# Edge scatter of a four-layer graph network: places settled and handed over two chunks at a time instead of four

## The reference, cut to what matters

```python
bias = jnp.full((n, n), NEG, dtype=x.dtype)
bias = bias.at[diag, diag].set(0.0)
bias = bias.at[dst, src].set(edge_weight.astype(x.dtype))
...
scores = jnp.einsum('hnd,hmd->hnm', q, k) / np.sqrt(HEAD_DIM)
scores = scores + bias[None, :, :]
attn = jax.nn.softmax(scores, axis=-1)
```

## Time and profile before

| what | value |
|---|---|
| median of 3 runs | 583.27 us (582.19 to 585.47) |
| the profiled execution | 581.37 us, of which span 579.6 us |
| busy: PE, DVE, ACT, POOL | 530.0, 396.6, 225.9, 282.2 us |
| mean granted clock of TensorE | 0.973 |
| scatters (L387, POOL) | x68, 75.1 us busy, mean 1105 ns, idle before them 40.4 us |
| one-hot builds (L1131, L1132, DVE) | x68 each, 407 and 609 ns |
| marks (L1114, DVE) | x68, 609 ns |
| one-hot matmuls (L521, PE) | x544, 119.5 us |

### The profile page before, as it was taken

The page is one execution under the profiler, slowest core; times in us unless marked ns, Lnnn a source line. Parts: engine busy times, 40 slices in busy tenths (PEclk is TensorE's granted clock), DMA queues, the critical chain, the costliest instruction groups (busy, mean ns, idle before and its releaser), DMA issues.

```text
span 579.6 us, 7779 instructions
## 1 busy us (share of the span) xinstructions
PE 530.0 (91%) x2524; PEld 351.7 (61%) x2524; DVE 396.6 (68%) x939; ACT 225.9 (39%) x473; POOL 282.2 (49%) x271
## 2 busy tenths in 40 slices
PE   6999999999969999898899999997998997999880
PEld 2444444448845545666677888877876785555750
DVE  6996979999947769974676744464427626774846
ACT  2120530017227662574441233143534226765443
POOL 6557556668457777404342600066653654766000
PEclk8999999999989999998999999998999999999996
DMA  7940000000665210226632500028652852100001
GB/s 239 400 151 1 1 1 0 0 0 2 198 199 166 55 37 1 73 60 157 213 115 82 178 31 1 0 81 248 182 182 73 259 171 69 47 2 1 0 0 73
DMA packets 29913, 54.37 MB, mean 94 GB/s; under 512 B 4962, under 2 KB 6446, under 8 KB 29368
## 3 DMA queue, kind: packets, MB, share of 16 engines
q1 hardware_dynamic: 15964, 27.14, 15.0%
q0 software_dynamic: 11968, 19.96, 11.5%
q10 hardware_dynamic: 1948, 6.86, 3.5%
HBM read 51.78 MB, written 2.17 MB: 93 GB/s over the span
## 4 chain that ended last, share of the span: by engine, by line
PE 47%; DVE 10%; ACT 5%; POOL 5%; DMA 4%; issue 3%; ACTq 0%; DVEq 0%; POOLq 0%
PE bank L498 9%; PE bank L499 8%; PE bank L500 8%; PE bank L616 4%; PE bank L600 4%; PE bank L591 3%; POOL wl L346 3%; DMA wh<-w_o 2%; PE bank L693 2%; PE bank L691 2%; PE bank L692 2%; DVE h L1084 2%; DVE h L1083 1%; PE bank L568 1%; PE bank L484 1%
## 5 line engine op out<-in xcount | busy, mean ns | idle before, releaser
L346 POOL TENSOR_TENSOR wl<-wraw,wh 128x512 fp32r<-128x512 f32 (+1 forms) x78 | 105.4, 1372 | 81.1 <-ACT x L811 14.9
L521 PE MATMUL bank<-hot 128*128 128x512 bf16 x544 | 119.5, 383 | 2.5 <-DVE hot L1132 2.5
L521 PEld LDWEIGHTS bank<-hot 128*128 128x128 bf16 x544 | 53.5, 99 | 68.7 <-DVE hot L1132 4.1
L387 POOL DMA_INDIRECT edge_bias<-ewn,cell_at x68 | 75.1, 1105 | 40.4 <-issue 20.2
L498 PE MATMUL bank<-wh,tl 128*128 128x512 f32 x176 | 71.3, 405 | 0.6 <-DVE tl L1043 0.5
L499 PE MATMUL bank<-wl,th 128*128 128x512 f32 x176 | 69.4, 395 | 0.0
L500 PE MATMUL bank<-wh,th 128*128 128x512 f32 x176 | 69.4, 394 | 0.0
L819 ACT ACTIVATE sp<-sp,peak 128x512 f32<-128x512 f32 x44 | 31.8, 722 | 26.4 <-DVE peak L1255 26.1
L1132 DVE TENSOR_SCALAR hot<-iota,pair_dst,digit 128x1024 bf16<-128x1024 f16 x68 | 41.4, 609 | 0.0
L498 PEld LDWEIGHTS bank<-wh,tl 128*128 128x128 f32 x176 | 33.5, 190 | 11.8 <-issue 4.2
L1114 DVE SCALAR_TENSOR_TENSOR eq<-keyb,key,later 128x384 f16<-128x384 f16 (+1 forms) x68 | 39.8, 609 | 0.0
(11 more groups left out here) (194 smaller groups left out, 1072.2 us busy)
## 6 DMA issues: line engine op xcount, KB each, us to landing
wraw<-w SPq DMA_DIRECT2D x26, 256.0 KB
wh<-w POOLq DMA_DIRECT2D x6, 1024.0 KB, 6.1
keyb<-edge_keys ACTq DMA_DIRECT2D x4, 1088.0 KB, 11.4
wh<-w_rel POOLq DMA_DIRECT2D x4, 1024.0 KB, 5.8
wraw<-w_rel SPq DMA_DIRECT2D x16, 256.0 KB
wraw<-w_qkv SPq DMA_DIRECT2D x8, 256.0 KB
wraw<-w_o SPq DMA_DIRECT2D x8, 256.0 KB
wh<-w_o POOLq DMA_DIRECT2D x2, 1024.0 KB, 8.0
```

The lines of the kernel that those rows point to most:

```text
L346: pool.tensor_tensor(wl[n % WSLOTS][:, k, 0:width], wraw[:, q % 3, 0:width], wh[n % WSLOTS][:, k, 0:width], ALU.subtract).then_inc(s["w_lo ...
L387: pool.indirect_dma_start(out=bias_dram, out_offset=bass.IndirectOffsetOnAxis(ap=cell_at[:, c:c + 1], axis=0), in_=ewn[:, c:c + 1], in_off ...
L521: mm = pe.matmul(ps(name)[:], hot[:, slot, 0, i * P:(i + 1) * P], hot[:, slot, 1 + kind, :], start=False, stop=last, skip_group_check=True)
```

## The change

Places are settled for two chunks at a time. In `build_and_place` the first two chunks of a group are settled behind the build of slot 2, the other two where all four were settled before. In the code between and behind the loops a settle stands behind each second mark. `dups` is raised at each second mark, and GpSimd waits for `placed` ahead of each second scatter. So 34 settles of two columns stand in place of 17 of four.

```diff
@@ GpSimd
             for c in range(CHUNKS):
-                if c % GROUP == 0:
-                    pool.wait_ge(s["placed"], c // GROUP + 1)
+                if c % 2 == 0:
+                    pool.wait_ge(s["placed"], c // 2 + 1)
                 if c >= WINDOW:
                     pool.wait_ge(scattered[c % WINDOW], 16 * (c // WINDOW))
@@ VectorE
             def mark(c, k):
 
                 ins = later_same(c + k, k)
-                if k == GROUP - 1:
+                if k % 2 == 1:
                     ins.then_inc(s["dups"], 1)
 
-            def settle(c, group):
-
-                dve.wait_ge(s["dups"], group + 1)
-                dve.scalar_tensor_tensor(out=cell_at[:, bass.ds(c, GROUP)], in0=dup[:, bass.ds(c, GROUP)], scalar=OUT_OF_RANGE,
-                                         in1=key[:, bass.ds(c, GROUP)], op0=ALU.mult, op1=ALU.add).then_inc(s["placed"], 1)
+            def settle(c, group, half):
+
+                dve.wait_ge(s["dups"], group * 2 + (half + 1))
+                at = c + 2 * half
+                dve.scalar_tensor_tensor(out=cell_at[:, bass.ds(at, 2)], in0=dup[:, bass.ds(at, 2)], scalar=OUT_OF_RANGE,
+                                         in1=key[:, bass.ds(at, 2)], op0=ALU.mult, op1=ALU.add).then_inc(s["placed"], 1)
@@ build_and_place
                     build_chunk(at + (first + slot), slot)
+                    if slot == 2:
+                        settle(c, group, 0)
                     mark(c, slot)
                 mark(c, RING - 1)
                 dve.wait_ge(s[f"hot_used{sweep}"], at)
                 build_chunk(at + (first + RING - 1), RING - 1)
-                settle(c, group)
+                settle(c, group, 1)
@@ between the loops
             for k in range(GROUP):
                 mark(behind, k)
-            settle(behind, behind // GROUP)
+                if k % 2:
+                    settle(behind, behind // GROUP, k // 2)
@@ behind the second loop
             for c in range(behind + CBLOCKS[1] * RING, CHUNKS, GROUP):
                 for k in range(GROUP):
                     mark(c, k)
-                settle(c, c // GROUP)
+                    if k % 2:
+                        settle(c, c // GROUP, k // 2)
```

## The result

The changed kernel took 579.92 us (median of 20 runs, 575.76 to 584.59 but for one run of 676.88 us), the kernel before, on the same chip, 583.28 us (20 runs). The ratio is 0.9931 with a 95% interval of 0.9908 to 0.9955, which is 4.0 us less (the medians differ by 3.4 us). The profiled execution took 581.01 us, of which 579.3 us are span.

A forecast was written before the change was run, and what follows sets the result against it. The end of GpSimd's scatters was taken to set the attention's start. 2.1 us from the scatters plus 0.5 us from TensorE's clock made 2.6 us off 583.27 us: 580.7 us, range 578.4 to 582.9 us.

The forecast's parts named there:

- rival A: The forecast itself: 1.5 to 3.5 us gained, 579.8 to 581.8 us; chance 0.50.
- rival B: Last scatters fall out of step with VectorE's counts, or the low clock goes wholly: likelier 3.5 to 5.5 us; chance 0.20.
- The 4.26 us: GpSimd's "issue" wait ahead of the load of `w_o`: taken to hang on the bias's landing and move along.
- Rival D: The 4.26 us wait ends at a fixed place and takes up the gain: 0 to 0.5 us, about 583.2 us; chance 0.12.
- The scatters: GpSimd's last scatters, freed by an earlier settle, end 2.1 us earlier; bounds 1.3 and 4.7 us.
- A gain of 2.1 us passes whole: From the scatters' end to the attention's first `scale_rows`: the whole 2.1 us arrives, being under the 4.7 us limit.
- 4.7 us of room: Before the attention: `scale_rows` could start 4.7 us earlier before TensorE's last product of v and first inverse limit it.
- The clock: TensorE's low clock at the attention's start: less work at half pace, 0.5 us gained; bounds 0 and 1.9 us.
- VectorE's settles: 17 more settles on VectorE: hidden in the loops' waits; counts and q start 0.1 to 0.2 us later.
- My sign for a higher price: One-hot matmuls ending more than 0.5 us later than about 129.8 us would show VectorE pays more than said.
- Rival C: Scatters among VectorE's builds: the two moved and the next two pay 0.5 us each, about 582.5 us; chance 0.14.
- Rival E: The settle in the loop body holds VectorE up, 1.2 us a round: slower, 586.7 us; chance 0.04.

The follow-up runs named there:

- padded change: The changed kernel with 112 more GpSimd semaphore increments that nobody waits for, making its program 128 instructions longer than the kernel before: ratio 0.9948.
- pads in both directions: Unread GpSimd increments added: 112 to the changed kernel (wait back, ratio 0.9948), 16 to the kernel before (wait gone, 0.9929).
- kernel with settles and waits: The changed kernel's two-chunk settles and 16 added GpSimd waits, but waiting for the same counts as before, so no scatter freed earlier: ratio 1.0023.
- kernel with more settles and no earlier scatters: The changed kernel's two-chunk settles with no scatter freed earlier: ratios 1.0061 and 1.0013 with GpSimd's old waits, 1.0023 with 16 more waits.
- waits alone: The kernel before with GpSimd waiting for `placed` ahead of each second scatter, for counts already there, and no added settles: ratios 0.9911 and 0.9953.
- moving the banks: VectorE reads count banks 4 to 7 before unpacking them: in the changed kernel 0.9943; in the kernel before with the 16 waits 0.9897 (577.92 us).
- before plus 16: The kernel before with 16 GpSimd semaphore increments that nobody waits for, between two pieces of its first `low`: ratio 0.9929.
- kernel with the first loop as before: The changed kernel with the first loop settled four chunks at a time as before, and as many GpSimd waits as the change: ratio 0.9938.

## Why the prediction was right, and where not

The forecast was 580.7 us, 0.45% less; measured were 0.69% less, inside the range of 578.4 to 582.9 us. The forecast of the median was 0.8 us off (579.92 us measured), but the size came out near by other steps, so its closeness is in part luck. The median lies at the lower edge of rival A, the 4.0 us of the ratio in the likelier part of rival B (3.5 to 5.5 us), and both things that B named happened: scatters got faster, and the low clock went wholly.

| scatters / GpSimd's fetch | behind the bias's load | moved out of its way |
|---|---|---|
| as before | 1 | 0.9929; 0.9911, 0.9953 |
| as before, with the added settles | 1.0061, 1.0013 | 1.0023 |
| freed earlier, with the added settles | 0.9948 | 0.9931, 0.9933 |

Against the kernel before, each of the two alone gives 0.5 to 0.9%, and both together no more. The padded change is the kernel that the forecast described: earlier scatters, and the wait still there. It gave 0.5% (0.1 to 0.9), where 0.45% was forecast.

- **The 4.26 us: wrong, and the main miss.** The step was "so I take the wait to hang on that landing, and to move along". It went with GpSimd's own instruction fetch, and the change moved the place of that fetch in the program by 16 instructions. I wrote that each second scatter's wait costs "nothing"; as waits that is so, but as instructions they took 4.3 us out. Rival D (a fixed place) had the same flaw: both moved or held the wait, neither removed it. That GpSimd's program length decides is shown, by the pads in both directions. That the packet is what GpSimd waits for is inferred, from its place in each case and from the 1.50 us that always lie between its end and the next instruction: no record links the two. That it takes long because of the bias's load is argued only: no run changed that load.
- **The scatters: right in mechanism, too small.** The first half was settled 1.87 us ahead of the second (1.94 said). But the last 12 also ran faster, 17.5 us in place of 19.0: four of 1.50 us in a row, and only 0.97 to 1.14 us in the eight others. Measured against the one-hot matmuls the end came 3.5 us earlier, not 2.1. In the span's own time it was 1.8 us, only because the sweeps were 1.7 us late in that execution.
- **"A gain of 2.1 us passes whole", "4.7 us of room": wrong.** The room was not fixed. The earlier `low` pieces fell on a count of VectorE that stands ahead of a bank read that k needs, and v came 1.8 us later. Of the 7.9 us at `w_o` 3.0 us passed. What I had named as the limit above ("TensorE's last product of v") was the bound.
- **The clock:** I took 0.5 us, with 1.9 us as the bound if no work runs low. TensorE's idle time shrank to 0.51 us and the clock did not fall there, so this came out at its bound, in both profiles. The reading behind the 0.5 us was sound: in the kernel with settles and waits the idle time was 3.32 us and one low stretch of 3.4 us followed (180.2 to 183.6 us), as expected for 3.3 us. What failed is the idle time that it was given.
- **VectorE's settles:** 0.1 to 0.2 us were said. The second sweep lasts as long as before (62.0 us from first to last weight load in both), and the first is within what it varies by. My sign for a higher price, one-hot matmuls more than 0.5 us later, did appear (1.7 us), but the second profile of the kernel before has them 3.3 us later than its first: the sign could not tell. What I had not costed is their shift against the scatters: it shows only where no scatter is freed earlier, as one scatter of 3.9 us.
- **Rival C:** the moved scatters took 1.14 and 1.10 us, not 0.5 us each more. Rival E: no held-up loop; the kernel with more settles and no earlier scatters is slower by 0.1 to 0.6%, of which only the 0.6 is clear of its interval, and what its profiles show of it is in the tail. For the count of 4.76 us beside three `low` pieces the Trainium skill ("SBUF — State Buffer", "Who interferes with whom") has a rule that fits: a VectorE instruction with two SBUF inputs contends with a GpSimd instruction that reads SBUF. For the 3.9 us scatter it does not settle the matter: the same section tells of a probe in which `tensor_tensor` did not stall a DMA, while here a scatter took 3.90 and 3.91 us beside four of them, in all three profiles with settles and no earlier scatter.
- Of my tests, "`w_o` near 152.4 us" and "TensorE's idle time is near 3.2 us" failed, on the good side: 148.30 and 0.51 us. "Last scatter ends at 141.5 to 142.4" held (142.27), but only since the later sweeps and the faster scatters cancelled.

What stays open: why VectorE stalls for 1 to 8 us between 46 and 61 us in all these kernels, and the end of the sweeps moves by up to 5.4 us between two executions of one program (135.5 and 130.1 us with the waits alone); why the vanished wait gives no time where the settles stand and no scatter is earlier; and whether moving the banks gains, which needs finer timing than 0.4%.

## What to carry to other kernels

A gap labelled "issue" in front of an instruction that waits for nothing may be the engine's own program arriving: look in the DMA rows for an instruction packet just ahead of its end, and compare with a build that has a few dummy instructions more before you credit a change with a gain. Any edit that adds or drops an instruction on that engine can move such a fetch in or out of a large load's way; here 16 increments were worth as much as the whole change. And room on another engine is not a constant: before you pass a gain on, ask what the work that starts earlier will now lie beside.

## What the runs showed of the hardware

- An 8 KB instruction packet that moved while a 1 MB load issued by GpSimd was under way went with 4.26 to 4.55 us of standstill on GpSimd, which ended 1.50 to 1.51 us after the packet (five profiles). Where it moved ahead of the load there was none (nine profiles). The two places differ by 16 instructions of the program, and 128 instructions more in all bring the standstill back.
- At the start of the attention, where TensorE had been idle for 0.51 to 0.99 us its clock stayed at 2.4 GHz; behind 2.48 us (before plus 16) and 3.32 us (settles and waits) it fell to 1.2 GHz for 3.4 us, behind 1.42 us (the first profile of the waits alone) it did so too, but only at 177.8 us, 1.4 us after TensorE was back; behind 5.35 us it was low for 6.9 us.
- At the later layer TensorE was idle 1.98 us before and 1.96 us after, and the low stretch behind it lasted 3.4 us in one and 6.9 us in the other. In the kernel with the first loop as before it was idle 1.98 us there too, and the clock stayed at 2.4 GHz (granted clock 1.00 from 243.8 to 250 us). The length of the idle time alone does not tell which.
